# The last three attention turns of a cross-attention and mixture-of-experts kernel: order of the output projection, PSUM banks, who normalises, and when the step table is sent

## The reference

```
x = x + Wo @ attention(q = rope(Wq LN(x)), k = rope(Wk ctx), v = Wv ctx) + bo     # 8 heads of 16 channels, 512 x 512 scores
h = LN(x)                                    # 2048 tokens of 512 numbers
logits = h @ gate.T                          # 32 experts
w = softmax(top_8(logits)), zero elsewhere
out = x + sum_e w_e * down_e( silu(h @ gate_e) * (h @ up_e) )     # inner width 192
```

## Time and profile before

| | |
|---|---|
| median of three runs | 1113.05 us |
| span of the profiled execution, first to last instruction | 1115.7 us |
| attention, until the rows of the last batch are scattered | until 543.5 us |
| from there to the first transpose of expert rows on PE | 543.5 to 554.6 us |
| experts | 554.6 us to the end |
| PE busy, of the span | 1007.8 us (90%) |
| DVE / ACT / POOL busy | 713.2 / 775.1 / 736.9 us |
| mean granted clock of PE, of full speed | 0.950 |

### The profile page before, as it was taken

One profiled execution on the slowest core, in us unless ns is written; L12 is line 12 of the kernel. 1 busy time (PEld: TensorE's weight loads), 2 busy tenths in 40 slices (PEclk: granted clock), 3 DMA queues, 4 the chain that ended last, 5 costly groups with the idle time before them and its releaser, 6 DMA issues.

```text
span 1115.7 us, 29688 instructions
## 1 busy us (share of the span) xinstructions
PE 1007.8 (90%) x7192; PEld 481.3 (43%) x7193; DVE 713.2 (64%) x1354; ACT 775.1 (69%) x1800; POOL 736.9 (66%) x663
## 2 busy tenths in 40 slices
PE   6589999999999999973199999999999999999996
PEld 2122222222222222221066666666666666666663
DVE  7878899999999888756434445544545553553521
ACT  2178888888888887662166676777677767777674
POOL 3034477777777774456557777778777777778775
PEclk9599999999999999886599999999999999999998
DMA  7313444444444333310187888898798898889674
GB/s 237 120 56 107 125 127 126 127 126 128 126 127 127 117 112 120 111 39 20 43 285 177 230 225 214 206 230 229 173 238 224 203 221 223 210 198 235 123 141 87
DMA packets 88882, 175.58 MB, mean 157 GB/s; under 512 B 23658, under 2 KB 40426, under 8 KB 84594
## 3 DMA queue, kind: packets, MB, share of 16 engines
q0 software_dynamic: 38080, 75.58, 31.5%
q1 hardware_dynamic: 50736, 99.26, 28.0%
q10 hardware_dynamic: 4, 0.02, 0.0%
HBM read 118.30 MB, written 61.58 MB: 161 GB/s over the span
## 4 chain that ended last, share of the span: by engine, by line
PE 42%; issue 3%; DVEq 2%; DVE 2%; DMA 1%; ACTq 1%; POOL 1%; ACT 0%; POOLq 0%; SPq 0%
PE ps L1697 23%; PE ps L1705 5%; PE ps L1723 2%; PE ps L1726 2%; PE ps L1724 2%; PE ps L1727 2%; PE ps L1725 2%; DVEq L349 1%; PE ps L1713 1%; DVE w_lo L1352 1%; PE ps L1715 1%; PE ps L1714 1%; ACTq L349 1%; DVE w_hi L1347 1%; POOL expert_rows L600 0%
## 5 line engine op out<-in xcount | busy, mean ns | idle before, releaser
L1036 DVE TENSOR_REDUCE mx<-ps 128x2 f32<-128x1024 f32 x256 | 303.7, 1222 | 37.3 <-PE ps L1669 34.4
L1697 PE MATMUL ps<-w_hi,o_raw 128*128 x1200 | 318.2, 327 | 0.0
L767 ACT ACTIVATE pr<-ps 128x512 f32<-128x512 f32 x512 | 278.4, 602 | 49.8 <-PE ps L1646 48.6
L741 POOL DMA_INDIRECT out<-v,s_idx x148 | 250.4, 1692 | 86.5 <-issue 40.3
L723 POOL DMA_INDIRECT pr<-normalised_tokens,g_idx x155 | 168.8, 1089 | 61.6 <-issue 18.2
L1697 PE MATMUL ps<-w_lo,o_raw 128*128 x600 | 196.2, 327 | 0.0
L757 ACT ACTIVATE o_raw<-ps 128x1024 f16<-128x1024 f16 (+1 forms) x183 | 174.9, 956 | 3.0 <-PE ps L1658 1.6
L1364 DVE SCALAR_TENSOR_TENSOR rope_b<-rope_a,stacks,ps 128x192 f32<-128x192 f32 x150 | 61.6, 411 | 147.9 <-ACT rope_a L923 108.0
L1697 PEld LDWEIGHTS ps<-w_hi,o_raw 128*128 128x128 f16 x1200 | 117.7, 98 | 85.8 <-issue 1.0
L600 POOL DMA_INDIRECT expert_rows<-rows,rowi x128 | 127.1, 993 | 37.2 <-issue 36.8
L1658 PE MATMUL ps<-pr,v 128*32 128x512 f32 x1024 | 140.3, 621 | 1.6 <-ACT pr L767 1.2
(11 more groups left out here) (161 smaller groups left out, 1464.0 us busy)
## 6 DMA issues: line engine op xcount, KB each, us to landing
stage<-in_expert_w SPq DMA_DIRECT2D x32, 1280.0 KB
stacks<-qk_parts SPq DMA_DIRECT2D x128, 96.0 KB, 2.7
w_lo<-in_x SPq DMA_DIRECT2D x32, 256.0 KB, 2.9
w_lo<-in_ctx SPq DMA_DIRECT2D x32, 256.0 KB, 5.8
qk_parts<-qk SPq DMA_DIRECT2D x32, 256.0 KB
qk_parts<-qk SPq DMA_DIRECT2D x32, 128.0 KB
out<-x SPq DMA_DIRECT2D x16, 256.0 KB, 4.9
normalised_tokens<-x2s SPq DMA_DIRECT2D x16, 256.0 KB, 2.5
```

The costliest lines, as they stand in the source:

```text
L741: nc.gpsimd.indirect_dma_start(out_rows, bass.IndirectOffsetOnAxis(s_idx[:, s.slot(4), 0:1], 0), y_sb[:, s.slot(4), :], None, bounds_check ...
L767: nc.scalar.activation(pr[:, n % 8, :], bank(f"s{n}"), ACT.Exp, scale=DH ** -0.5).then_inc(exp_done, 1)
L1036: V.tensor_reduce(mx[:, b.slot(2), at:at + 3:2, tile], bank(f"m{n}"), AXX, ALU.max).then_inc(mx_done, 1)
L1697: last = mm(ps[:, s.slot(2), 0:2 * INTER], xt[:, s.slot(2), at:at + P], w[:, cols], start=(m == 0), stop=(m == 3 * KT - 1))
```

## The change

In turn 15 and after:
- the logits and the counts of the last three batches get a bank of their own (`v_bank[0][:, 1, :]`, 32 columns from 0 and 64 columns from 128), the transposed tokens of the last two batches get `s_bank[2]`;
- the output projection is issued in its two halves (`output_of(b, g)`), each after its own half of `on_done`, with scores, logits or counts in between;
- for batches 14 and 15, DVE adds epsilon, subtracts the mean and multiplies by the inverse deviation, and makes the low part; POOL does the power alone; the shift is gone. The orders of PE, DVE, ACT and POOL in turns 15 to 17 are rewritten around it; `first_weights` moves behind the plan;
- SP sends the step table and loads it back before it waits for the scattered rows;
- `sums` waits for the counts of batch 12 only.

In the expert steps: POOL's `add` reads two values of the table of earlier adds, raises them to at least 0 in registers, and waits for those two and for the third add back outright. The loads of `LAST_GROUP` (each engine), `NEXT` (SP) and `SPLIT` (DVE) no longer pass the reason that leaves the run-time bounds check out.

```diff
+        def among_last(b, n):
+
+            return isinstance(b.k, int) and b.count(1) >= NB - n
+
+        def logits_bank(b):
+            return v_bank[0][:, 1, :] if among_last(b, 3) else bank("lg")[:, 0, :]
+
+        def counts_bank(b):
+            return v_bank[0][:, 1, P:] if among_last(b, 3) else bank("cnt")[:, 0, :]
+
+        def tokens_bank(b):
+            return s_bank[2] if among_last(b, 2) else bank("xt")
...
+            if waited:
+                return nc.values_load_multi_w_load_instructions(view, engines=[eng.engine], min_val=lo, max_val=hi)[1]
...
             batch_turns(sp, turn)
+            sp.wait_ge(plan_sem, TABLE_STEPS)
+            sp.dma_start(steps_d.rearrange("(q p) f -> p q f", p=P), stepi[:, :, :]).then_inc(tab_out, 16)
+            sp.wait_ge(tab_out, 16)
+            sp.dma_start(tab[:, :], steps_d[0:STEPS + SEEN, :].rearrange("(o s) f -> o (s f)", o=1)).then_inc(tab_in, 16)
             for p in range(2):
...
+                def inverse_deviation(b):
+                    gp.wait_ge(vare_done[1], b.count(1, 1))
+                    gp.wait_ge(xn2_done, b.count(1))
+                    apart(gp)
+                    nc.gpsimd.tensor_tensor(rstd[:, 1:2], vare[:, 1:2], half[:, :], ALU.pow).then_inc(rstd2, 1)
...
                 if turn_no == NB - 1:
                     normalised_x2(br)
+                    scatter_rows(bs, (0, 1))
                     low_of_x2(br)
-                    scatter_rows(bs, (0, 1, 2))
-                    normalised_x2(bo)
-                    scatter_rows(bs, (3, 4, 5, 6, 7))
-                    low_of_x2(bo)
-                    scatter_rows(br, (0, 1, 2, 3, 4, 5, 6, 7))
+                    scatter_rows(bs, (2, 3, 4, 5, 6, 7))
+                    inverse_deviation(bo)
                     return
                 if turn_no == NB:
-                    normalised_x2(bo)
-                    scatter_rows(br, (0,))
-                    low_of_x2(bo)
-                    scatter_rows(br, (1, 2, 3, 4, 5, 6, 7))
+                    scatter_rows(bs, (0, 1, 2, 3, 4, 5, 6, 7))
+                    scatter_rows(br, (0, 1))
+                    inverse_deviation(bo)
+                    scatter_rows(br, (2, 3, 4, 5, 6, 7))
...
+                one, two = (s + -1).slot(4), (s + -2).slot(4)
+                first = min(one, two)
+                before = fields(gp, s, first, 2, 16 * (STEPS // 4 + 1), abs(one - two), table=before_tab, width=4)
+                for held, v in zip(at_least_none, before):
+                    gp.reg_alu(held, v, 0, ALU.max)
                 gp.wait_ge(s_set, s.count(1, 1))
                 gp.wait_ge(y_out, s.count(1, 1))
-                for q in range(4):
-                    gp.wait_ge(added[q], before[q])
+                need(gp, added[(s + -3).slot(4)], (s + -3).rounds(4, 16, 32))
+                for q, adds in zip(sorted((one, two)), at_least_none):
+                    gp.wait_ge(added[q], adds)
...
+                    exponentials(9, 8)
                     read_xt()
-                    exponentials(14, 4)
+                    exponentials(17, 1)
                     read_o(b2, 0)
-                    exponentials(18, 3)
-                    normal_x2(bo)
-                    exponentials(21, 1)
+                    exponentials(18, 5)
+                    exponentials_of_top()
+                    exponentials(23, 6)
                     high_of_x2(bo)
-                    exponentials(22, 4)
+                    exponentials(29, 3)
+                    return
+                if turn_no == NB:
+                    read_xt()
+                    read_o(bo, 1)
                     exponentials_of_top()
-                    exponentials(26, 6)
-                    return
-                if turn_no == NB:
-                    read_o(bo, 1)
-                    read_xt()
-                    exponentials_of_top()
-                    normal_x2(bo)
                     high_of_x2(bo)
                     return
...
+                def variance_of_x2(b):
+                    dve.wait_ge(stat2, b.count(2, 2))
+                    dve.wait_ge(rstd2, b.count(1))
+                    V.tensor_scalar(vare[:, 1:2], mv[:, 1, 1:2], EPS, None, ALU.add).then_inc(vare_done[1], 1)
+
+                def normal_x2(b):
+                    dve.wait_ge(rstd2, b.count(1, 1))
+                    dve.wait_ge(x2_lo, b.count(1))
+                    V.tensor_scalar(xn2[:, :], x2[:, b.slot(2), :], mv[:, 1, 0:1], rstd[:, 1:2], ALU.subtract, ALU.mult).then_inc(xn2_done, 1)
+
+                def low_of_x2(b):
+                    dve.wait_ge(x2_hi, b.count(1, 1))
+                    dve.wait_ge(tok_stored[b.slot(2)], b.rounds(2, 16, 0))
+                    V.tensor_tensor(x2s[:, b.slot(2), LO, :], xn2[:, :], x2s[:, b.slot(2), HI, :], ALU.subtract).then_inc(x2_lo, 1)
+
                 if turn_no == NB - 1:
                     over_sums(bo, 0)
                     over_sums(bo, 1)
+                    link = choice(br)
                     residual(bo)
                     stats_of_x2(bo)
+                    variance_of_x2(bo)
+                    weights(br, link)
+                    normal_x2(bo)
+                    read_counts(br)
+                    places(br, link)
+                    low_of_x2(bo)
+                    over_sums(bo + 1, 0)
+                    return
+                if turn_no == NB:
+                    link = choice(br)
+                    over_sums(bo, 1)
+                    weights(br, link)
+                    read_counts(br)
+                    places(br, link)
+                    residual(bo)
+                    stats_of_x2(bo)
+                    variance_of_x2(bo)
+                    normal_x2(bo)
+                    low_of_x2(bo)
+                    return
...
+            first_weights()
             dve.wait_ge(tab_in, 16)
...
+            def output_of(b, g):
+                pe.wait_ge(on_done, b.count(2, g + 1))
+                part = mm(bank("y")[:, 0, :], ow[:, g, :], o_n[:, g, :], start=(g == 0), stop=(g == 1))
+                if g == 1:
+                    part.then_inc(y_mm, 1)
...
-                pe.wait_ge(cnt_done, b.count(2, -2))
+                pe.wait_ge(cnt_done, 2 * (NB - 3))
...
-                    pe.wait_ge(lg_done, NB - 3)
-                    pe.wait_ge(mx_done, 16 * NB)
-                    pe.wait_ge(x2_done, NB - 2)
-                    output(bo)
+                    pv(2)
+                    s(14)
                     bank_is_free(pe, it, "xt")
                     tokens_transposed(br)
-                    pv(2)
-                    s(14)
-                    pe.wait_ge(x2_done, NB - 1)
-                    logits(br)
                     s(16)
                     pv(3)
                     s(18)
+                    pe.wait_ge(lg_done, NB - 3)
+                    pe.wait_ge(x2_done, NB - 2)
+                    output_of(bo, 0)
                     s(20)
+                    logits(br)
+                    output_of(bo, 1)
+                    s(22)
                     pv(4)
-                    s(22)
-                    pe.wait_ge(on_done, bo.count(2, 2))
-                    bank_is_free(pe, it, "cnt")
+                    s(24)
                     counts_of(br)
-                    s(24)
                     pv(5)
                     s(26)
                     s(28)
                     sums(b2, 0)
                     pv(6)
                     s(30)
+                    pe.wait_ge(exp_done, b2.count(32, 30))
+                    tokens_transposed(bo)
                     return
                 if turn_no == NB:
                     pv(7)
-                    bank_is_free(pe, it, "xt")
-                    tokens_transposed(br)
-                    sums(bo, 1)
                     pe.wait_ge(lg_done, NB - 2)
                     logits(br)
-                    bank_is_free(pe, it, "y")
-                    output(bo)
-                    bank_is_free(pe, it, "cnt")
+                    sums(bo, 1)
+                    pe.wait_ge(x2_done, NB - 1)
+                    output_of(bo, 0)
+                    pe.wait_ge(cnt_done, 2 * (NB - 2))
+                    counts_of(br)
+                    output_of(bo, 1)
+                    return
+                if turn_no == NB + 1:
+                    pe.wait_ge(xt_read, NB - 1)
+                    tokens_transposed(br)
+                    pe.wait_ge(lg_done, NB - 1)
+                    logits(br)
+                    pe.wait_ge(cnt_done, 2 * (NB - 1))
```

More of the change, by code:

```diff
@@ L332, in step_loop @@
                 body(Turn(n // GROUP, n % GROUP, GROUP, STEPS))
-            last, = fields(eng, Turn(0, 0, GROUP, STEPS), LAST_GROUP, 1, STEPS // GROUP - 1, lo=FEWEST // GROUP - 1)
+            last, = fields(eng, Turn(0, 0, GROUP, STEPS), LAST_GROUP, 1, STEPS // GROUP - 1, lo=FEWEST // GROUP - 1, waited=True)
             with eng.Fori(1, STEPS // GROUP, 1) as i:
@@ L339, in step_loop, with fields @@
```

(31 more changed lines are left out.)

21 lines of the change are left out of this document (8 added, 13 removed).

## The result

The changed kernel takes 1112.54 us (median of 13 executions, 1108.77 to 1116.26); the kernel before, on the same chip, 1119.22 (13 executions, 1111.85 to 1120.71). The ratio is 0.996, 95% interval 0.9941 to 0.9979: faster by 0.4%, where 1100.4 us, 1.1% faster, was forecast. 1112.5 lies above the range. The profiled execution after is the one of 1112.54, span 1110.8; in every execution whose span is on record the time is the span plus 1.7 to 1.85.

What follows compares the result with a forecast made beforehand. PE bounds the expert steps; the loss lies in the chain of waits before them, begun by turn 15's stall. Gain 15.4 at the step start less 2.8 for checks is 12.6; 1113.05 - 12.6 = 1100.4 us, range 1096 to 1107.

Steps and rivals of the forecast that it cites:

- This execution is 2.65 above the median, which I take off: Whole kernel: the profiled execution was taken as 2.65 us above the median, so gains were subtracted from 1113.05 us.
- I take 0.4, near the register operations: Expert steps: DVE's checked reads of four SPLIT values cost 0.4 us at each of seven group starts, 2.8 us lost.
- Rival (a): Expert steps: each bound check is a compare with a branch, 5.6 us lost over seven groups, total 1103.3; chance 0.15.
- The start of the steps: First row index copied at 534.4 instead of 549.80: 12.4 us from earlier scatters plus 3.0 from the step table.
- Turn 15 without the stall: Turn 15: half projections placed among the scores remove ACT's idle 5.60 us; exponentials end at 496.5, 5.9 us earlier.
- Normalising on DVE: Batch 15: power ends at 510.7, DVE's subtraction takes 0.4 and low part 0.69; tokens ready at 512.6, before at 523.1.
- Last scatter: POOL's eight scatters of batch 15: the last at 529.0, landed at 531.1, against 543.5 before, 12.4 us earlier.
- Step table early: Before the steps: SP's two step-table transfers, 3.75 us, end at 527.7 under the scatters; gain 3.0 us.
- Rival (c): Checks cost nothing seen and POOL's order does not bite: gain 15.4 + 1, total 1096.7 us; chance 0.12.
- (b): Turn 15 doesn't tighten, ACT still ends near 502.4: 4.6 us of the 15.4 stay, total 1105.0; chance 0.13.
- (d): Something else holds the step start, rows of 15 no earlier, only the table's 3.0 us gained: 1110 to 1113; chance 0.06.
- Rival (e): Expert steps: DVE's check makes reads sequential, 4.0 us a group, 28 for seven, total 1125.7, slower; chance 0.04.

Runs made afterwards that it cites:

- f: Kernel before with the change's expert-step edits, SPLIT unchecked and raised to 0 once, and the step table sent early: 1116.28 us, 0.9992 of before.
- o: The changed kernel, unaltered, measured again beside other kernels: 1111.22 us, 0.9944 of before.
- n: Kernel of l with batch 14's projection whole again and in its old place in turn 15: 1107.31 us, 0.9894 of before.
- k: a_clamp with one scatter of batch 14 instead of two ahead of POOL's power in turn 16: 1105.10 us, 0.9886 of before.
- m: Kernel of l with DVE's first_weights held until the last scatters have landed: 1099.11 us, 0.9833 of before.
- e: a_clamp with the step table sent where it was before, behind the row table's first load: 1106.82 us, 0.9917 of before.
- d: Changed kernel with each SPLIT value checked a second time, against a bound one lower: 1148.47 us, 1.0071 of before, on a slower chip.
- l: a_clamp with DVE's reads of four ROW values behind the issue of the weight split's first half: 1099.60 us, 0.9843 of before.
- a_clamp: Changed kernel with DVE's SPLIT values unchecked, the used one raised to 0 in its branch: 1130.62 us, 0.9911 of before, on a slower chip.

## Why the prediction was wrong, by its steps

Forecast 1100.4, measured 1112.5: 12.1 us, in three parts that add up to it.

*"This execution is 2.65 above the median, which I take off"*: 4.4 us. This is the step of the sum that failed at its base. A span of 1115.7 is an execution of 1117.4, by time and clock with the slower group; the three times shown were two of the quicker group and one of the slower, and their median, 1113.05, was 6.2 under that of all 13 (1119.22). The gain was worked out from the slower execution's stalls and subtracted from the quicker group's time. The 3.75 of the projection is at half the clock (1.96 in f) and the 5.60 of idle time with it (3.39 in f), so the quicker executions have less to give back. 1117.4 - 1113.05 = 4.4.

*"I take 0.4, near the register operations"*: 4.8 us. The mechanism was the right one, DVE's read on the chain at a group start, and the size wrong in both factors. A group pays 0.53 from the product to the split (4.25, 609.33 to 613.58, against 3.72 before, 621.26 to 624.98), which is near 0.4, but the loss is 7.56 against 2.8. By the distances between the transposes the seven group starts lose 4.2 together, 0.6 each, and six further steps, which the chain of before did not name, 4.0. The sign that the prediction gave for being wrong, PE under 99% busy in the steps, came true: 532.2 of 540 is 98.6%. Rival (a) had the operation's kind (a compare of each bound) and a better size, 5.6; its total missed by the base. The Trainium skill (Advanced Engine Details and Errata, Control Flow Timing) prices a compare-and-branch; the check is no branch here but a fused register operation of 183 ns and an assertion of 23. By eight branches to a group it gave 6.0 for the seven, nearer than the forecast, but for another operation.

*The start of the steps, "gain 15.4"*: 12.46, 2.9 short. 1.4 of it is that turn 15 began 1.37 later in the execution after than in that of before. Ahead of it the clock fell twice in both, but the first fall lasted longer after (0.69 from 424 to 430 us, where before had 0.97 from 423 to 430), and across it the lag grew from 0.35 to 1.78. In o, the same code, it never fell (turn 15's transpose at 466.13 instead of 472.39). Counted from there, the steps of the prediction hold:
- Turn 15 without the stall, 496.5 + 1.4 = 497.9: the exponentials end at 497.83. Right, and n shows that it was this stall.
- Normalising on DVE, tokens ready at 512.6 + 1.4 = 514.0: the low part ends at 514.79, transposed at 514.93. Right to 0.9. The power ends at 512.76 where 510.7 + 1.4 was expected, and the subtraction takes 0.61, not 0.4. The power waits behind a scatter, as said. But the rows of 14 were ready 0.9 early (507.04), and 2.21 us of idle time on POOL before the second scatter, which the prediction does not have, used that up: that the sum still came near is in part luck. That an earlier power doesn't matter (k) was not seen.
- Rows of 15 at 519.2 + 1.4 = 520.6: 521.21. 0.6 late.
- Last scatter: 1.0 later than worked out in its start, and 2.97 to landing instead of 2.12. It took 1.81 because DVE's scaling of the first weights (530.81 to 532.37) ran beside it; "first_weights behind the plan, hidden" was right for DVE and PE and wrong for POOL. m shows it: 0.7 us. The Trainium skill (SBUF — State Buffer, Who interferes with whom) says that such a scaling, in a 2-port mode, locks GpSimd out for the whole instruction. The trace agrees: the scaling, 2560 columns in 1.56 us, begins ahead of the scatter, ends at 532.37, and the scatter 0.83 behind it. k's scatter beside the two-tensor split (526.17 to 529.00) took 2.56 and ended 0.83 behind that. The prediction cited the rule for the small low part, which cost the scatter beside it 0.4 (1.35 at 514.28), and not for the 1.56 us that the change moves on to the scatters.
- Step table early, 3.0: it is home before the last scatter (ACT's sequencer reads it from 529.6 on). Its price is 4.2 to 4.4 by e's front, 3.9 by e's chain.
- Row table 2.54 to land, as before.

Rival (c), "POOL's order does not bite", was half true. Rivals (b) and (d) fall: turn 15 tightened and the rows of 15 came 8.5 us earlier. The measured 1112.5 lies in (d)'s 1110 to 1113 by chance. Rival (e), the serialised reads, has the right place and asked for 2.2 us a group; d with doubled checks shows that side of it, 1.0071 of before, with steps 23 us longer than before's.

## What to carry to other kernels

Before a gain is taken from one execution, look at whether the times fall in groups, which group the profiled one is in, and what the granted clock was in the stretch that is to be tightened: a stall is dearer where the clock fell in it (5.60 us against 3.39 here). A busy share of 99.8% is no proof that nothing is left: the distance between repeats of one instruction showed 2.9 us where the busy time showed 0.9. A check on a value just read costs its sequencer time in series, so on the engine that sets the pace check once at the use or not in the chain, and put reads behind the issue of a long instruction. When work is moved to a later time, list what runs there on the engines that share a port with it, as well as what waits for it.

## What the runs showed of the hardware

- The granted clock falls to 1.2 GHz in turns 13 to 15 in some executions and not in others of the same code (after: 0.50 in 418 to 424; o: full from 400 to 496). From 400 to 410 us PE was busy 9.07 of 10 us at the full clock in before, after and f alike; then it fell in the first two and not in f. What decides it is not in these traces.
- A check on a value read into a register takes DVE's sequencer 183 + 23 ns in series, four values 1.13 us.
- A scatter's issue on POOL takes 0.96 us alone and 1.81 or 2.56 where DVE splits weights beside it (after, k); with DVE held back it is 0.96 (m).
- POOL is idle for 2.21 us before the second scatter of batch 14 in turn 16, with nothing that the profile shows to wait for, the same 2.21 in after, e, l and a_clamp; in k it stands behind the power (2.81). It was not explained.
- The slower chip took 1141.56 us at the median for the kernel whose medians elsewhere are 1112.74, 1119.08 and 1119.22; its turn-15 transpose of the maxima was at 486 to 488 instead of 466 to 473. Ratios were comparable across chips, times were not.
